# A two-stage float32 product of eight elements, its second stage in part by seven block products in place of eight

## The chip, the cores and the metric

The kernel runs on one core of one Trainium2 chip (trn2). The metric is device time in microseconds (us), the median of several runs. One execution of it is also taken by the hardware profiler, which gives the page and the trace read here.

## What is computed

There are NB = 8 batch elements of T = 256 tokens and D = 1024 channels, all in float32. Cut to what matters, with `w` the 1024 x 1024 weight that an id picks for each element out of eight:

```
y      = einsum('bsi,boi->bso', x, weight[adapter_ids])        # stage 1
base   = einsum('btd,od->bto', y, base_W) + base_b             # stage 2, the base
logits = einsum('btd,nd->btn', y, router_W) + router_b         # 15 router columns
probs  = softmax(logits); top 8 of 15, each added to its expert -> gate[b, t, e]
h      = einsum('btd,erd->bter', y, A)                         # 8 experts x 16 = 128 columns
out    = x + base + einsum('bter,eor->bto', h * gate, B) * 2.0
```

## The kernel before

**Split in two parts.** A float32 product is made of three passes in the type float32r. ScalarE (ACT) casts a raw tile to a high part, VectorE (DVE) subtracts that from the raw tile and gets the low part, and TensorE (PE) multiplies high by high, high by low and low by high into the same PSUM bank.

**Stage 1.** For each element, 8 chunks of 128 output channels (`stage1_chunk`, L540). A chunk is 8 pairs of matmuls, one over 512 columns (the weight's high part against the high and the low part of x, L546) and one over 256 (its low part against x's high part, L548), into `y_ps`. ACT then copies half of the bank to `y_part` (L300), DVE adds the two halves to `y_sum` (L468), ACT casts `y_hi` (L306), DVE makes `y_lo` (L397). The weights of a chunk are 512 KB; the SP queue loads them into one of four slots `w_raw`, as soon as DVE has made the low part of the chunk that was there (`w_lo_done`, L198). ACT casts them (L293), DVE makes `w_lo` (L385).

**Stage 2.** The shared matrix has AR + D = 144 + 1024 = 1168 columns: 128 of A, 15 of the router and one of padding, then the base. It lies in SBUF in two parts (`s2_hi`, `s2_lo`) for the whole run, and is cut in three groups of 384, 392 and 392 columns. `group` (L563) makes one group for one of the two token tiles of 128 tokens: 8 k-slices of three matmuls, 24 in all. `stage2` (L593) sets the order on PE:

```
group(b, 0, 0, ...); group(b, 1, 0, first).then_inc(ar_done, 1)
group(b, 0, 1, first); group(b, 0, 2, first)
pe.wait_ge(hw_done, b + 1)          # then the two transposes of hw
group(b, 1, 1, first)
pe.wait_ge(hwt_lo_done, b + 1)      # then lora_b for five groups, group(b, 1, 2), lora_b(1, 2)
```

When `ar_done` comes, DVE runs `routing` (L404): logits, softmax, top 8, gates, and `hw`, the gated A columns. PE transposes `hw`, ACT and DVE split it, and `lora_b` (L583) adds the product with B, 18 matmuls an element. DVE adds each group to `res` (`output`, L463), which holds x plus the bias (L448), and SP stores it.

**Order.** Every engine's program is written out by hand, for the first element, a hardware loop over elements 1 to 6, and the last. DVE's for an element (L471) is: for each chunk `y_sum`, a `w_lo`, `y_lo`; then the low parts of the next element's x (`x_lo`, L392), routing, the bias, `hwt_lo`, the output. The next element's x has a tile `x_raw` of its own, loaded at the element's start. In the first element the shared matrix is loaded piecewise through four slots `c_raw`, split by ACT (L285) and DVE (L379), and the first two chunks of stage 1 run in plain float32 (L560) straight from the raw tiles.

Of the kernel before, what the change touches and what calls it, by code (L numbers as in the profile page):

```python
# [19 lines left out]
C_SLOTS = 4  # L33
LORA_SCALE = 32.0 / 16.0
WARM_UP = 10
MARK = 3.0e38


def adaln_ffn_kernel(nc, xT, x, ids, wT, a_t, base_t, b_t, router_t, base_b, router_b, expert_map, out):
# [23 lines left out]
    with ExitStack() as ctx:  # L63
        def sb(name, shape, dt=F32):
            return ctx.enter_context(nc.sbuf_tensor(name, shape, dt))

        def sem(name):
            return ctx.enter_context(nc.semaphore(name))


# [615 lines left out]
```

## Time and profile before

| what | value |
|---|---|
| time, median of 3 runs | 422.53 us (422.02 to 422.95) |
| span of the profiled execution, first to last instruction | 421.1 us |
| PE busy | 413.3 us, 98% of the span |
| DVE busy | 220.0 us, 52% |
| ACT busy | 135.3 us, 32% |
| DMA queue, share of 16 engines | 43.4% |

The page gives the profiled execution by its span; the time of a run is taken around the program, and the median lies 1.4 us above the span. An element takes 50.7 us, of which stage 1 is some 22 and stage 2 some 28. Engines overlap: a busy share tells how full an engine is, not what the time waits for, and to see that one reads the idle time of the engine that is full. The notation is L for a line of the kernel, `out<-in` for the tiles, `<-` for who ended an idle time.

### The profile page before, as it was taken

How to read it: one execution, taken by the hardware profiler on the slowest of the kernel's cores; microseconds unless marked ns; L12 is line 12 of the kernel's file. 1: busy time of each engine (PE TensorE's matmuls, PEld its weight loads, DVE VectorE, ACT ScalarE, POOL GpSimd, SP SyncE). 2: the span in 40 equal slices, each digit the busy share in tenths (PEclk: the TensorE clock that was granted, in tenths of full speed). 3: DMA queues.
4: the chain of work that ended last, by engine and by line, in shares of the span. 5: the costliest groups of instructions: out<-in, count | busy, mean ns of one | idle time of the engine just before them, and what ended most of it. 6: DMA issues, size and time to landing. Idle time of an engine off the chain costs nothing.

```text
span 421.1 us, 6443 instructions
## 1 busy us (share of the span) xinstructions
PE 413.3 (98%) x2356; PEld 390.4 (93%) x2356; DVE 220.0 (52%) x438; ACT 135.3 (32%) x236; POOL 0.8 (0%) x8
## 2 busy tenths in 40 slices
PE   6989999999999999999999999999999999999997
PEld 5879998899988999899998999989998899988996
DVE  2577858654266623676227652366424655255232
ACT  3475534630055300561015600365004540053000
POOL 0000000000000000000000000000000000000000
PEclk8999999999999999999999999999999999999999
DMA  6876966930177203771057511574016740150002
GB/s 201 287 281 215 362 238 255 339 128 0 69 252 283 95 0 121 270 256 50 0 191 269 196 42 50 194 280 173 0 50 224 280 144 0 50 199 2 0 2 100
DMA packets 20093, 64.72 MB, mean 154 GB/s; under 512 B 2418, under 2 KB 6130, under 8 KB 19186
## 3 DMA queue, kind: packets, MB, share of 16 engines
q1 hardware_dynamic: 20082, 64.57, 43.4%
q8 instruction: 7, 0.11, 0.1%
q14 instruction: 4, 0.03, 0.0%
HBM read 56.18 MB, written 8.39 MB: 153 GB/s over the span
## 4 chain that ended last, share of the span: by engine, by line
PE 95%; DMA 2%; DVE 1%; SPq 0%; ACT 0%; issue 0%
PE y_ps L546 26%; PE s_ps L578 16%; PE s_ps L577 16%; PE s_ps L580 16%; PE y_ps L548 13%; DMA w_raw<-in_wT 2%; PE y_ps L560 2%; PE s_ps L589 2%; PE s_ps L588 2%; PE s_ps L590 2%; PE s_ps L605 0%; DVE w_lo L385 0%; ACT s_hi L285 0%; SPq L195 0%; SPq L191 0%
## 5 line engine op out<-in xcount | busy, mean ns | idle before, releaser
L546 PE MATMUL y_ps<-x_split,w_hi 128*128 128x512 f32 x496 | 172.7, 392 | 1.2 <-DVE w_lo L385 1.2
L548 PE MATMUL y_ps<-x_split,w_lo 128*128 128x256 f32 x496 | 139.1, 280 | 0.0
L577 PE MATMUL s_ps<-s_hi,y_hi 128*128 128x392 f32 (+1 forms) x384 | 131.2, 342 | 0.0
L578 PE MATMUL s_ps<-s_lo,y_hi 128*128 128x392 f32 (+1 forms) x384 | 130.4, 340 | 0.0
L580 PE MATMUL s_ps<-s_hi,y_lo 128*128 128x392 f32 (+1 forms) x384 | 130.0, 339 | 0.0
L546 PEld LDWEIGHTS y_ps<-x_split,w_hi 128*128 128x128 f32 x496 | 92.9, 187 | 21.6 <-DVE w_lo L385 1.5
L548 PEld LDWEIGHTS y_ps<-x_split,w_lo 128*128 128x128 f32 x496 | 94.0, 190 | 0.0
L385 DVE TENSOR_TENSOR w_lo<-w_raw,w_hi 128x1024 fp32r<-128x1024 f32 x62 | 75.2, 1215 | 1.4 <-ACT w_hi L293 1.4
L577 PEld LDWEIGHTS s_ps<-s_hi,y_hi 128*128 128x128 f32 x384 | 72.2, 188 | 0.3
L578 PEld LDWEIGHTS s_ps<-s_lo,y_hi 128*128 128x128 f32 x384 | 72.2, 188 | 0.0
L580 PEld LDWEIGHTS s_ps<-s_hi,y_lo 128*128 128x128 f32 x384 | 72.1, 188 | 0.0
L300 ACT COPY y_part<-y_ps 128x256 f32<-128x256 f32 x62 | 23.0, 371 | 148.5 <-PE y_ps L548 148.5
L293 ACT CAST w_hi<-w_raw 128x1024 fp32r<-128x1024 f32 x62 | 64.9, 1053 | 4.8 <-DMA w_raw<-in_wT 4.7
L468 DVE TENSOR_TENSOR y_sum<-y_ps,y_part 128x256 f32<-128x256 f32 x62 | 26.3, 424 | 59.6 <-ACT y_part L300 59.3
L463 DVE TENSOR_TENSOR res<-s_ps,res 128x392 f32<-128x392 f32 (+1 forms) x48 | 23.2, 510 | 57.0 <-PE s_ps L590 56.3
L397 DVE TENSOR_TENSOR y_lo<-y_sum,y_hi 128x256 fp32r<-128x256 f32 x64 | 26.8, 419 | 9.0 <-ACT y_hi L306 8.9
L306 ACT CAST y_hi<-y_sum 128x256 fp32r<-128x256 f32 x64 | 26.0, 407 | 12.8 <-DVE y_sum L468 7.9
L448 DVE TENSOR_TENSOR res<-res,bias 128x1024 f32<-128x1024 f32 x16 | 18.9, 1217 | 5.0 <-DMA res<-in_x 5.0
L321 ACT CAST hwt_hi<-s_ps 128x256 fp32r<-128x256 f32 x8 | 3.0, 375 | 54.6 <-PE s_ps L605 54.6
L392 DVE TENSOR_TENSOR x_split<-x_raw,x_split 128x1024 fp32r<-128x1024 f32 x14 | 16.6, 1220 | 2.0 <-ACT x_split L313 2.0
L452 DVE TENSOR_TENSOR hwt_lo<-s_ps,hwt_hi 128x256 fp32r<-128x256 f32 x8 | 3.4, 425 | 26.7 <-ACT hwt_hi L321 26.7
L589 PE MATMUL s_ps<-b_lo,hwt_hi 128*128 128x392 f32 (+1 forms) x48 | 15.3, 320 | 0.0
(46 smaller groups left out, 162.5 us busy)
## 6 DMA issues: line engine op xcount, KB each, us to landing
w_raw<-in_wT SPq DMA_DIRECT2D x63, 512.0 KB, 3.5
res<-in_x SPq DMA_DIRECT2D x16, 512.0 KB, 4.9
out<-res SPq DMA_DIRECT2D x15, 512.0 KB, 2.7
x_raw<-in_xT SPq DMA_DIRECT2D x7, 1024.0 KB, 5.5
c_raw<-in_base_t SPq DMA_DIRECT2D x8, 392.0 KB, 3.7
x_raw<-in_xT SPq DMA_DIRECT2D x4, 256.0 KB, 4.2
c_raw<-in_base_t SPq DMA_DIRECT2D x2, 480.0 KB, 7.4
w_raw<-in_wT SPq DMA_DIRECT2D x4, 128.0 KB, 4.4
```

What stands on the lines that cost most here:

```text
L293: nc.scalar.copy(w_hi[:, slot, :, :], w_raw[:, slot, :, :]).then_inc(w_hi_done, 1)
L306: nc.scalar.copy(y_hi[:, o, :], y_sum[:, o % 2, :]).then_inc(y_hi_done, 1)
L385: nc.vector.tensor_tensor(w_lo[:, slot, :, :], w_raw[:, slot, :, :], w_hi[:, slot, :, :], ALU.subtract).then_inc(w_lo_done, 1)
L397: nc.vector.tensor_tensor(y_lo[:, o, :], y_sum[:, o % 2, :], y_hi[:, o, :], ALU.subtract).then_inc(y_lo_done, 1)
L463: nc.vector.tensor_tensor(res[:, t, cols], s2_ps[:, g, t, skip:skip + OUT[g + 1] - OUT[g]], res[:, t, cols], ALU.add).then_inc(out_done, 1)
L468: nc.vector.tensor_tensor(y_sum[:, o % 2, :], y_ps[:, o % 2, 0:T], y_part[:, o % 2, :], ALU.add).then_inc(y_sum_done, 1)
L546: nc.tensor.matmul(y_ps[:, o % 2, :], w_hi[:, slot, k, :], x_split[:, k, :, :].rearrange("p s t -> p (s t)"), start=(k == 0), stop=False)
L548: mm = nc.tensor.matmul(y_ps[:, o % 2, 0:T], w_lo[:, slot, k, :], x_split[:, k, 0, :], start=False, stop=(k == KC - 1))
L577: nc.tensor.matmul(dst, hi, s2_hi[:, k, cols], start=(k == 0), stop=False)
L578: nc.tensor.matmul(dst, hi, s2_lo[:, k, cols], start=False, stop=False)
L580: mm = nc.tensor.matmul(dst, lo, s2_hi[:, k, cols], start=False, stop=(g == 0 and k == KC - 1))
L589: nc.tensor.matmul(dst, hwt_hi[:, t, :], b_lo[:, cols], start=False, stop=False, skip_group_check=skip)
```

## The change

**The base columns.** 288 of the 1024 base columns stay as they are, behind the 144 columns of A and router: `plain` (24 matmuls of 432 columns for each token tile). The other 736 are two halves N1 and N2 of 368. With the eight k-slices cut in two halves of four, and the tokens in two tiles, this is a 2 x 2 by 2 x 2 block product. From the second element on it is made by seven block products instead of eight (Winograd's form), each of 12 matmuls of 368 columns:

- on the left, sums of blocks of y: S1 = y10 + y11, S2 = S1 - y00, S3 = y00 - y10, S4 = y01 - S2 (here y10 is tile 1, first half of k), made by DVE in every element and split by ACT and DVE like y;
- on the right, sums of blocks of the base: T1 = B01 - B00, T2 = B11 - T1, T3 = B11 - B01, T4 = B10 - T2, made once, behind the first element;
- products that enter several outputs stay in a PSUM bank (`x_ps`) and are read by DVE between two products that add to it, so PE waits for DVE's `add` there.

The first element uses plain blocks: its blocks are B00, B10, T1 and B11, so that N2 is made as T1 and B11 products on one bank; it has the same columns as before.

**Bytes.** Raw tiles now lie on the bytes of the low parts: `w_raw` on `w_lo`, the next x on the low half of `x_split`, `y_sum` on `y_lo`. So a weight slot is free when PE is through with the chunk (`y_ps_done`), no longer when DVE is, and the next x is loaded when stage 1 is over.

**Order.** The y chunks come in the order 0, 4, 1, 5, ... and y is cast in pairs. The bias is added ahead of the routing.

The core of the diff:

```
-                    sp.wait_ge(w_lo_done, split(b, 3 + o))
-                    load_w(...)
+                    sp.wait_ge(y_ps_done, OC * b + c + 1)
+                    load_w(this if c + W_SLOTS < OC else nxt, (c + W_SLOTS) % OC)
...
+                if not last:
+                    load_x(b + 1)            # behind the last chunk, 2 x 512 KB
...
+            def sums(b, j):
+                nc.vector.tensor_tensor(s_raw[:, j, S1, :], y10, y11, ALU.add).then_inc(s1_done, 1)
+                nc.vector.tensor_tensor(s_raw[:, j, S3, :], y00, y10, ALU.subtract)
+                dve.wait_ge(s1_done, KH * (b - 1) + j + 1)
+                nc.vector.tensor_tensor(s_raw[:, j, S2, :], s_raw[:, j, S1, :], y00, ALU.subtract).then_inc(s_done, 1)
...
+            def fourth(b):
+                dve.wait_ge(ar_done, 2 * b + 1)
+                dve.wait_ge(s_lo_done, KH * (b - 1) + KH)
+                ... S4 in three operations of 512 elements, then fourth_hi on ACT, fourth_lo on DVE
...
+            def element(b, last=False):                      # DVE
+                for c in range(OC):
+                    make_y_sum(b, c)
+                    if c % 2:
+                        sums(b, c // 2)
+                        make_y_lo(b, c // 2)
+                    adapter_lo(b, c + 3)
+                    if c % 2:
+                        sums_lo(b, c // 2)
+                if isinstance(b, int) and b == 1:
+                    t2_lo()                                  # 1472 elements
+                    t34_lo()                                 # 2944 elements
+                add_bias(b)
+                fourth(b)
+                if not last:
+                    make_x_lo(b + 1)
+                fourth_lo(b)
+                stage2(b)          # routing_logits, add x_ps, routing_gates, the other adds
...
+            def stage2(b):                                   # PE
+                plain(b, 1)
+                plain(b, 0)
+                product(x_ps, y_block(0, 0), B00).then_inc(x_ps_done, 1)
+                pe.wait_ge(t_lo_done, 3)
+                product(z_ps, s_block(S1), T1).then_inc(z_ps_done, 1)
+                pe.wait_ge(x_added, x_adds(b, 1))
+                product(x_ps, s_block(S2), T2, begins=False).then_inc(x_ps_done, 1)
+                pe.wait_ge(hw_done, b + 1)
+                transposes()
+                product(w_ps, y_block(1, 0), B10)
+                pe.wait_ge(x_added, x_adds(b, 2))
+                product(x_ps, s_block(S3), T3, begins=False).then_inc(x_ps_done, 1)
+                pe.wait_ge(s4_lo_done, b)
+                product(z_ps, y_block(0, 1), B11, begins=False)
+                ... lora_b, then product(x_ps, y_block(1, 1), T4, begins=False)
```

Three places show what moves. **First, DVE in the loop over elements**, from the last low part of weights to the first use of the logits. Before:

```order
L385 TENSOR_TENSOR w_lo<-w_raw,w_hi 128x1024 [waits w_hi_done]
L391 ISA
L392 TENSOR_TENSOR x_split<-x_raw,x_split 128x4x256 [waits x_hi_done]
L391 REGISTER_ALU
L392 TENSOR_TENSOR x_split<-x_raw,x_split 128x4x256 [waits x_hi_done]
L407 REGISTER_ALU
L408 TENSOR_TENSOR logits<-s2_ps,router_bias 128x30 [waits ar_done]
```

Now:

```order
L487 TENSOR_TENSOR s_lo_70<-s_raw_71,s_hi_69 128x384 [waits s_hi_done]
L554 ISA
L555 TENSOR_TENSOR res_74<-res_74,bias_73 128x1024 [waits res_in0]
L555 TENSOR_TENSOR res_74<-res_74,bias_73 128x1024 [waits res_in1]
L490 ISA
L492 TENSOR_TENSOR y_sum_67<-y_hi_65,s_hi_69 128x4x128 [waits s_lo_done,ar_done]
L493 TENSOR_TENSOR s4_tmp_68<-y_lo_66,s_lo_70 128x4x128
L495 TENSOR_TENSOR y_sum_67<-y_sum_67,s4_tmp_68 128x4x128 [waits s4_part_done]
L464 TENSOR_TENSOR x_split_52<-x_raw_53,x_split_52 128x4x256 [waits x_hi_done]
L463 REGISTER_ALU
L464 TENSOR_TENSOR x_split_52<-x_raw_53,x_split_52 128x4x256 [waits x_hi_done]
L499 TENSOR_TENSOR y_lo_66<-y_sum_67,y_hi_65 128x4x128 [waits s4_hi_done]
L507 TENSOR_TENSOR logits_85<-pl_ps,router_bias_82 128x30 [waits ar_done]
```

Two additions of the bias and four operations for S4 now stand between the last low part and the logits.

**Second, PE in the same loop**, where the third group before, and the products on `z_ps` and `x_ps` now, begin behind a wait. Before:

```order
L580 MATMUL s2_ps<-s2_hi,y_lo 128x392
L566 REGISTER_ALU
L577 MATMUL s2_ps<-s2_hi,y_hi 128x392 [waits out_done]
```

Now:

```order
L816 ISA [waits t_lo_done]
L817 REGISTER_ALU [waits s_lo_done]
L761 MATMUL z_ps<-st_hi_57,s_hi_69 128x368 [waits z_added]
...
L819 REGISTER_ALU
L761 MATMUL x_ps<-st_hi_57,s_hi_69 128x368 [waits x_added]
...
L821 REGISTER_ALU
L781 MATMUL v_ps<-ident_80,hw_77 128x128 [waits v_added,hw_done]
```

`out_done` was a wait for the output of the element before; `x_added` is one for an `add` of this element.

**Third, DVE behind stage 1 of the first element**, from the last `y_lo` to `hwt_lo` (the rows of the routing left out). Now:

```order
L606 TENSOR_TENSOR st_lo_58<-hi_raw_60,st_hi_57 128x2x2x368 [waits blocks_hi_done]
...
L625 TENSOR_TENSOR hi_raw_60<-hi_raw_60 128x4x368 [waits mask_done]
L627 TENSOR_TENSOR st_raw_59<-st_raw_59,hi_raw_60 128x4x368 [waits t_done]
L555 TENSOR_TENSOR res_74<-res_74,bias_73 128x1024 [waits res_in0]
...
L542 TENSOR_TENSOR hw_77<-pl_ps,gate_n_96 128x256 [waits gate_done]
L464 TENSOR_TENSOR x_split_52<-x_raw_53,x_split_52 128x4x256 [waits x_hi_done] x2
L697 TENSOR_TENSOR b_lo_62<-b_raw_63,b_hi_61 128x1024 [waits b_hi_done]
L458 TENSOR_TENSOR w_lo_50<-w_raw_51,w_hi_49 128x1024 [waits w_hi_done] x3
L549 TENSOR_TENSOR hwt_lo_76<-v_ps,hwt_hi_75 128x256 [waits hwt_hi_done]
```

Before, `hw` was followed by `b_lo`, one half of x and `hwt_lo` at once:

```order
L440 TENSOR_TENSOR hw<-s2_ps,gate_n 128x256 [waits gate_done]
L379 TENSOR_TENSOR b_lo<-c_raw,b_hi 128x1024 [waits c_hi_done]
L392 TENSOR_TENSOR x_split<-x_raw,x_split 128x4x256 [waits x_hi_done]
L452 TENSOR_TENSOR hwt_lo<-s2_ps,hwt_hi 128x256 [waits hwt_hi_done]
```

The second half of x and the three low parts of weights moved ahead of `hwt_lo`, and block sums and the bias ahead of the routing.

## Rows read from the trace of the kernel before

**Rows 1.** The page: span, and busy time of each engine

```profile
span 421.1 us, 6443 instructions
PE 413.3 (98%) x2356; PEld 390.4 (93%) x2356; DVE 220.0 (52%) x438; ACT 135.3 (32%) x236; POOL 0.8 (0%) x8
```

**Rows 2.** The page: the chain that ended last, share of the span by engine

```profile
PE 95%; DMA 2%; DVE 1%; SPq 0%; ACT 0%; issue 0%
```

**Rows 3.** Stretches: length, then busy (count) of PE, PEld, DVE, ACT, POOL, clock, DMA

```profile
7.49:16.04 8.55, 8.55 (x32) 7.16 (x32) 3.11 (x5) 3.53 (x5) 0.00 (x0) 0.80 0.87 301
16.04:66.00 49.96, 48.77 (x279) 45.95 (x278) 36.82 (x71) 25.11 (x38) 0.00 (x0) 1.00 0.75 263
...
265.80:316.50 50.70, 50.70 (x294) 48.06 (x293) 26.18 (x52) 15.62 (x28) 0.00 (x0) 1.00 0.40 145
```

**Rows 4.** PE in time, one element: start us, us, line, operation, out<-in, count

```profile
237.32 0.33 PE L577 MATMUL s_ps<-s_hi,y_hi 128*128 128x384 f32 x1
...
245.71 0.34 PE L577 MATMUL s_ps<-s_hi,y_hi 128*128 128x392 f32 x1
...
261.03 0.34 PE L577 MATMUL s_ps<-s_hi,y_hi 128*128 128x392 f32 x1
...
265.11 0.34 PE L580 MATMUL s_ps<-s_hi,y_lo 128*128 128x392 f32 x1
...
265.82 0.40 PE L546 MATMUL y_ps<-x_split,w_hi 128*128 128x512 f32 x1
```

**Rows 5.** DVE in time, the same element

```profile
237.92 0.42 DVE L468 TENSOR_TENSOR y_sum<-y_ps,y_part 128x256 f32<-128x256 f32 x1 [0.88 <-ACT y_part L300]
...
240.72 2.36 DVE L392 TENSOR_TENSOR x_split<-x_raw,x_split 128x1024 fp32r<-128x1024 f32 x2 [0.34 <-ACT x_split L313]
...
245.92 0.19 DVE L408 TENSOR_TENSOR logits<-s_ps,router_bias 128x30 f32<-128x30 f32 x1 [2.83 <-PE s_ps L580]
...
247.00 0.18 DVE L422 TENSOR_REDUCE row_sum<-prob 128x2 f32<-128x30 f32 x1
...
248.96 2.35 DVE L448 TENSOR_TENSOR res<-res,bias 128x1024 f32<-128x1024 f32 x2
```

**Rows 6.** ACT in time, the same element

```profile
237.52 0.37 ACT L300 COPY y_part<-y_ps 128x256 f32<-128x256 f32 x1 [1.15 <-PE y_ps L548]
238.38 0.41 ACT L306 CAST y_hi<-y_sum 128x256 fp32r<-128x256 f32 x1 [0.49 <-DVE y_sum L468]
238.69 1.05 ACT L293 CAST w_hi<-w_raw 128x1024 fp32r<-128x1024 f32 x1
```

**Rows 7.** Groups by line and form: count, busy us, mean ns, idle before

```profile
L463 DVE TENSOR_TENSOR res<-s_ps,res 128x392 f32<-128x392 f32 x32 | 17.7, 564 | 30.4 <-PE s_ps L590 29.6
...
L492 DVE TENSOR_TENSOR x_split<-x_raw,x_split 128x512 fp32r<-128x512 f32 x4 | 2.7, 693 | 7.7 <-ACT x_split L341 7.7
...
L341 ACT CAST x_split<-x_raw 128x512 fp32r<-128x512 f32 x4 | 2.5, 618 | 5.2 <-DMA x_raw<-in_xT 5.2
```

**Rows 8.** DVE in time, first element

```profile
45.75 0.70 DVE L521 TENSOR_SCALAR expert_mask<-map_f 128x15 f32<-128x15 f32 x8
```

**Rows 9.** PE in time, first element

```profile
7.49 0.89 PE L560 MATMUL y_ps<-x_raw,w_raw 128*128 128x256 f32 x2 [2.13 <-DMA w_raw<-in_wT]
...
25.99 0.50 PE L546 MATMUL y_ps<-x_split,w_hi 128*128 128x512 f32 x1 [1.19 <-DVE w_lo L385]
...
34.42 0.34 PE L577 MATMUL s_ps<-s_hi,y_hi 128*128 128x384 f32 x1
...
63.02 0.40 PE L546 MATMUL y_ps<-x_split,w_hi 128*128 128x512 f32 x1
```

**Rows 10.** DMA issues: count, KB each, us to landing

```profile
w_raw<-in_wT SPq DMA_DIRECT2D x63, 512.0 KB, 3.5
res<-in_x SPq DMA_DIRECT2D x16, 512.0 KB, 4.9
...
x_raw<-in_xT SPq DMA_DIRECT2D x7, 1024.0 KB, 5.5
```

More of the change, by code:

```diff
@@ L32 @@
 F32_CHUNKS = 2
-C_SLOTS = 4
 LORA_SCALE = 32.0 / 16.0
@@ L273, in _ @@
+            store(0, 1, slice(0, D))
             with sp.Fori(1, NB - 1) as b:
@@ L466, in make_y_sum, with add @@
[L466 to L486 removed]
+            def add(t, cols, ps):
+                return nc.vector.tensor_tensor(res[:, t, cols], ps, res[:, t, cols], ALU.add)
@@ new lines, in _ @@
+            blocks_lo(0)
+            blocks_lo(1)
+            masks()
+            block_sums_1_2()
+            add_bias(0)
+            routing_logits(0)
+            routing_gates(0)
+            make_x_lo(1)
+            dve.wait_ge(b_hi_done, 1)
+            nc.vector.tensor_tensor(b_lo[:, :], b_raw[:, :], b_hi[:, :], ALU.subtract).then_inc(b_lo_done, 1)
+            for c in range(OC, OC + 3):
+                adapter_lo(0, c)
+            make_hwt_lo(0)
+            block_sums_3_4()
+            dve.wait_ge(res_biased, 2)
@@ new lines, in _ @@
+            dve.wait_ge(z_ps_done, 1)
+            add(0, N2, z_ps[:, 0:NH]).then_inc(z_added, 1)
+            dve.wait_ge(x_ps_done, 1)
+            add(1, N2, x_ps[:, 0:NH]).then_inc(x_added, 1)
+            dve.wait_ge(w_ps_done, 1)
+            add(0, N1, w_ps[:, 0:NH]).then_inc(w_added, 1)
+            add_plain(0)
+            t1_lo()
+            dve.wait_ge(v_ps_done, 1)
+            add(1, N1, v_ps[:, 0:NH]).then_inc(v_added, 1)
+            element(1)
+            with dve.Fori(2, NB - 1) as b:
@@ new lines, in product @@
+            def product(ps, y_block, block_of, begins=True, wait_blocks=0):
+                dst = ps[:, 0:NH]
+                hi, lo = y_block
+                for j in range(KH):
+                    if wait_blocks and j % 2 == 0:
+                        pe.wait_ge(blocks_lo_done, j + wait_blocks)
+                    nc.tensor.matmul(dst, hi(j), st_hi[:, j, block_of, :], start=begins and j == 0, stop=False, skip_group_check=not begins)
+                    nc.tensor.matmul(dst, hi(j), st_lo[:, j, block_of, :], start=False, stop=False, skip_group_check=not begins)
+                    mm = nc.tensor.matmul(dst, lo(j), st_hi[:, j, block_of, :], start=False, stop=(j == KH - 1),
+                                          skip_group_check=not begins)
+                return mm
@@ new lines, in y_block, with s_block, lora_b @@
+            def y_block(half, t):
+                return [(lambda j, y=y: y[:, half * KH + j, t * P:(t + 1) * P]) for y in (y_hi, y_lo)]
+            def s_block(i):
+                return [(lambda j, s=s: s[:, j, i, :]) for s in (s_hi, s_lo)]
+            def lora_b(t, dst, cols, begins=False):
+                skip = not begins
+                nc.tensor.matmul(dst, hwt_hi[:, t, :], b_hi[:, cols], start=begins, stop=False, skip_group_check=skip)
+                nc.tensor.matmul(dst, hwt_hi[:, t, :], b_lo[:, cols], start=False, stop=False, skip_group_check=skip)
+                return nc.tensor.matmul(dst, hwt_lo[:, t, :], b_hi[:, cols], start=False, stop=True, skip_group_check=skip)
```

780 lines of the change are left out of this document (454 added, 326 removed).

## The prediction

> **What bounds the kernel now.** I read the page's busy times first: PE is busy for 413.3 of 421.1 us [rows 1], and the chain that ended last is 95% PE [rows 2]. Then the stretches: in an element of the loop PE is busy for 50.70 of 50.70 us at clock 1.00 (2.4 GHz), DVE for 26.2, ACT for 15.6 [rows 3]. So PE's columns set the time, and DVE has slack on average. The change takes columns from PE and hands DVE work, with waits for it, so the question is at what moment DVE's work is asked for. The view for that is the engines in order of time around the end of stage 1, at 237.32 us, which I call zero below [rows 4 to 6].
>
> **What it takes from PE.** Stage 2 lasts from 237.32 to 265.82, 28.50 us, so stage 1 takes 22.20 [rows 3, 4]. Its 48 matmuls of 384 columns take 8.39 us, 0.1748 each, and 23 of 392 columns take 4.08, 0.1774 each [rows 4]. That is 0.453 ns a column; I scale by it. A matmul of 432 columns then takes 0.1956, one of 368 takes 0.167, one of 288 some 0.131. Now: 48 x 0.1956 + 84 x 0.167 + 12 x 0.167 + 6 x 0.131 + 0.26 for the transposes = 9.39 + 14.03 + 2.00 + 0.79 + 0.26 = 26.47. Before, the same sum gives 8.39 + 17.03 + 2.13 + 0.66 + 0.26 = 28.47, as measured. So **2.0 us less in each of seven elements, 14.2 us in all**, if PE never waits. The first element keeps its columns.
>
> The Trainium skill (TensorE: Matmul & The Clock Gate, section on the back-to-back issue gap) has a matmul at full clock cost its columns at 2.4 GHz and some 2.5 ns. The trace disagrees by 12 ns on 392 columns (166 against 177). By that figure the seven elements would save 4416 columns and 12 matmuls each, 13.1 us, and the forecast would be 1.1 us higher.
>
> **What DVE must do in the loop before PE may go on.** The sixth product, S2 by T2, adds to the bank that the `add` on `x_ps` must first have read (L819 in the change). PE gets there after two `plain` and two products: 9.39 + 24 x 0.167 = 13.4 us. DVE's path to that `add`:
> - y_sum of the last chunk runs from 0.60 to 1.02 [rows 5]. Three sums of 128 elements: the nearest rows are 0.19 for 30 elements and 0.42 for 256 [rows 5], so I estimate 0.29 each; one waits for another, and y_lo starts at 1.8, over two chunks at once (512 elements: 0.69, or 0.61 to the next start [rows 7]), to 2.4.
> - ACT casts y at 1.06 (0.52 to the next start) and then weights for 1.05 [rows 6, 7]. So w_lo runs from 2.7 to 3.8 (two of this size take 2.36, 1.14 apart [rows 5]), the low part of the sums (384 elements, 0.48) to 4.3.
> - The bias, twice 1.14 [rows 5], to 6.5. S4: two operations of 0.61 and a third that waits for the second, to 8.5.
> - ACT casts S4 (0.5) and the first half of x (1.05), to 10.15. DVE takes both halves of x (2 x 1.14) to 12.4, S4's low part 0.6 to 13.0.
> - Logits to the first sum over probabilities take 247.00 - 245.92 = 1.08 [rows 5], to 14.1. The `add` of 368 elements takes 0.54 (0.564 for 392 [rows 7]), to 14.7.
>
> So **PE waits 14.7 - 13.4 = 1.3 us in each loop element**. Bounds: 0 if the small operations cost nothing and the casts overlap better, 2.5 if each of some ten new waits costs 0.1 more. The rest of the routing takes 248.96 - 247.00 = 1.96 [rows 5] and ends at 16.6; PE is through S2 by T2 at 16.7, so the transposes don't wait. What is late next is covered: the `add` on x_ps for S3 ends near 17.5 and is wanted at 18.9; hwt_lo at 18 is wanted at 23. S4's low part at 13.0 is wanted at 20.9. The next x is issued behind one weight load after zero; landed one after the other they take 3.5 + 5.5 = 9.0 us [rows 10], and ACT is ready for it at 9.1. In pieces a quarter as long that could cost up to 1 us; I take 0.
>
> Net for elements 2 to 6: 5 x (-2.03 + 1.3) = -3.65. The last has no next x (2.3 us of DVE and ACT's two casts gone from the path), so it does not wait: -2.0.
>
> **Element 1** has the block sums' low parts in the same path, ahead of the bias: 1472 and 2944 elements. From 512 to 1024 elements a DVE operation grows by 1.02 ns an element [rows 5, 7], so 1.6 and 3.1 us, with ACT's cast ending at 4.4 just ahead: the path moves by 4.85. PE waits 6.15: -2.03 + 6.15 = +4.1.
>
> **Element 0.** Stage 1 ended at 34.42, its chunk 5 having waited to 25.99 for weights [rows 9]. Now DVE and ACT have the plain part's split (1152 elements, 1.3 and 1.1 us) ahead of y_sum 4, on which chunk 6 waits: w_lo of 6 to about 28.2, split to 29.5, y_sum to 29.9, where chunk 6 could start near 28.3. I take +1.1, bounds -1.0 (A and router are loaded earlier, the old wait goes) and +2.5. In stage 2, counted from its start, DVE's work ends: four low parts of blocks of 1472 elements from 3.0 to 9.4, masks 0.9 (0.70 for the eight comparisons [rows 8]) to 10.3, two block sums to 13.6, bias to 15.9, routing (3.04 [rows 5]) to 18.9. PE wants `hw` after 9.39 + 48 x 0.167 = 17.4: it waits 1.5. Then two halves of x, b_lo and three w_lo, 6 x 1.14, and hwt_lo: 26.15. PE wants it at 18.95 + 0.26 + 4.0 = 23.2: it waits 2.9. Before, this stage took 28.6 without a stop [rows 9], so +4.4.
>
> **The clock.** Before, PE stood still for 2.1 us behind its warm-up, up to 7.49 [rows 9], and over the next 8.55 us the mean clock is 0.80, part of it thus at half clock (1.2 GHz), which loses 0.2 x 8.55 = 1.7. A stop of 1.2 us ahead of 25.99 [rows 9] left it at 1.00 [rows 3]. The 6.15 us of element 1 is far longer than the first, the 1.3 us stops are like the second. I put **+1.7** for one stretch at half clock; bounds 0 and 3.4 (element 0's 2.9 as well). The Trainium skill (TensorE: Matmul & The Clock Gate, Part 1) says that the throttled clock is the default state and activity releases it, a rule that speaks against any change that makes PE stop; both rows agree with it.
>
> **Sum.** 421.1 + 1.1 + 4.4 + 4.1 - 3.65 - 2.0 + 1.7 = 426.7 us of span. The tail behind the last matmul is alike (one add, one small store). The median stood 1.4 above the span: **428.1 us**, 5.6 slower. A measurement of this kernel tells some 0.2% (0.85 us) from no change.
>
> **Rivals.**
> - *DVE is in time in the loop.* If its path is shorter by 1.3 us, elements 2 to 6 never wait, and if the clock stays up too: 426.7 - 6.5 - 1.7 + 1.4 = 419.9, faster. For it: DVE is half idle. Against: every large operation on the path is priced by its own row. It decides from 1.3 us on; in between lie results near no change. Chance 0.16, of it 0.03 for the full 14.2 us (about 408), which would need element 0 and 1 covered too.
> - *Each short stop brings half clock.* Five more losses of up to 1.7: near 436. The skill's rule would allow it; the 1.2 us stop of before speaks against. 0.09.
> - *Weights come late.* A slot is now free when PE is through, three chunks (8.3 us) ahead. Landing 3.5, or 4.9 as for `res` beside other loads [rows 10], cast 1.05, low part 1.2, and about 1 us in both queues make 6.8 to 8.2. A wait of 1 us in each of seven elements gives 435. 0.08.
> - *The products are not fewer.* If PE's records don't drop by 84 from 2356, the saving is absent: 442. 0.01.
> - The forecast, with its own range of 425 to 431.5: 0.58. Near no change: 0.08.
>
> Faster 0.16, same 0.08 and slower 0.76 come from these; the range, 419.8 to 434.5, takes in the first rival and stops short of the second.
>
> **What would show it.** PE: 2272 matmuls; a wait on x_ps by the `add` (L558) of about 1.3 us in elements 2 to 6 and 6 us in element 1; waits for hw and hwt_lo of 1.5 and 2.9 in element 0; no wait for w_lo in the loop; one dip of the clock. Loop elements of 50.0 us, the last 48.7. If they take 48.7 as well, DVE's path is mis-sized; if they exceed 50.7, a new wait stands in stage 1 or the clock is down.

## The result and the profile after

The changed kernel takes **431.54 us** (median of 4 runs, 429.67 to 432.55), the kernel before 422.74 beside it (422.02 to 423.70). The ratio is 1.0204, 95% interval 1.0171 to 1.0236: slower by 2.0%, and the whole interval lies above 1. The forecast was 428.1 with a range of 419.8 to 434.5.

The page of the changed kernel, from its longest run of the four: span, busy times, clock in 40 slices, and chain by engine. They answer to [rows 1, 2].

```profile
span 430.7 us, 6373 instructions
...
PE 404.3 (94%) x2272; PEld 373.5 (87%) x2272; DVE 295.6 (69%) x577; ACT 154.9 (36%) x238; POOL 0.8 (0%) x8
...
PEclk9999999999599999999999999999999999999999
...
PE 61%; DVE 21%; ACT 6%; issue 6%; DMA 5%; SPq 1%; DVEq 0%; ACTq 0%
```

PE makes 2272 matmuls where it made 2356, and is busy for 404.3 us instead of 413.3. But its share of the span fell from 98% to 94% and its share of the chain from 95% to 61%, with 21% for DVE. One slice of the clock row shows a 5. Ahead of the products on `x_ps` (L761) PE stood idle for 12.5 us, until the `add` (L558) was done. The waits of PE, in total, times and the longest:

```profile
PE x_ps L761 <- DVE res L558: 12.5, 6, 6.8
PE y_ps L726 <- DVE y_sum L470: 2.9, 3, 1.4
PE z_ps L775 <- DVE hwt_lo L549: 2.8, 1, 2.8
...
PE v_ps L781 <- DVE hw L542: 1.6, 1, 1.6
```

Stretches, columns as in [rows 3]: stage 2 of the first element, stage 1 and stage 2 of element 1, and element 3:

```profile
35.20:68.48 33.28, 28.92 (x167) 27.99 (x165) 30.91 (x51) 16.35 (x16) 0.00 (x0) 1.00 0.42 162
68.48:91.95 23.47, 22.47 (x130) 19.41 (x130) 15.45 (x28) 12.26 (x21) 0.00 (x0) 1.00 0.66 225
91.95:128.48 36.53, 29.72 (x154) 28.67 (x153) 24.56 (x47) 6.99 (x11) 0.00 (x0) 0.86 0.18 59
178.92:228.93 50.01, 48.95 (x282) 45.44 (x282) 35.31 (x72) 17.92 (x29) 0.00 (x0) 1.00 0.42 147
```

Piece by piece, by the times at which PE begins each in both kernels (before: [rows 3, 9] and its other elements):

| piece | before, us | after, us | difference | forecast |
|---|---|---|---|---|
| up to stage 2 of element 0 | 34.42 | 35.20 | +0.78 | +1.1 |
| stage 2 of element 0 | 28.60 | 33.28 | +4.68 | +4.4 |
| element 1 | 50.70 | 60.00 | +9.30 | +4.1, and 1.7 for the clock |
| element 2 | 50.71 | 50.44 | -0.27 | -0.73 |
| elements 3 to 6 | 4 x 50.70 | 4 x 50.00 | -2.80 | -2.92 |
| element 7 and tail | 53.87 | 51.77 | -2.10 | -2.0 |
| span | 421.1 | 430.7 | +9.6 | +5.6 |

The table puts what is missing in one place, element 1. Here is DVE at the end of its stage 1, which ends at 91.95:

```profile
93.63 0.42 DVE L470 TENSOR_TENSOR y_sum<-y_ps,y_sum 128x256 f32<-128x256 f32 x1
...
97.43 1.69 DVE L646 TENSOR_TENSOR st_lo<-st_raw,st_hi 128x1472 fp32r<-128x1472 f32 x1
99.03 3.22 DVE L641 TENSOR_TENSOR st_lo<-st_raw,st_hi 128x2944 fp32r<-128x2944 f32 x1
102.17 2.35 DVE L555 TENSOR_TENSOR res<-res,bias 128x1024 f32<-128x1024 f32 x2
...
108.08 2.36 DVE L464 TENSOR_TENSOR x_split<-x_raw,x_split 128x1024 fp32r<-128x1024 f32 x2 [1.63 <-ACT x_split L367]
```

The low parts of T2 and of T3 and T4 (1.69 and 3.22 us) stand ahead of the bias, S4 and x. And PE from there on, as matmuls and as stretches:

```profile
112.54 0.68 PE L761 MATMUL x_ps<-st_hi,s_hi 128*128 128x368 f32 x1 [6.81 <-DVE res L558]
113.01 0.51 PE L762 MATMUL x_ps<-st_lo,s_hi 128*128 128x368 f32 x1
113.32 0.51 PE L763 MATMUL x_ps<-st_hi,s_lo 128*128 128x368 f32 x1
```

```profile
112.50:118.60 6.10, 6.06 (x20) 5.98 (x21) 3.22 (x11) 0.37 (x1) 0.00 (x0) 0.50 0.00 0
```

PE stands still for 6.81 us. Then the matmuls start 0.31 us apart instead of 0.167, and the granted clock is 0.50 (1.2 GHz) for 6.10 us (in the stretch behind it, up to 121.00, the mean is 0.99). The clock fell while PE stood still, not when it started again: the mean is 1.00 from 106.00 to 108.00, 0.60 in the next 2 us and 0.50 behind them.

The steady element does what the forecast had said step by step. Its stage 1 ends at 201.11:

```profile
205.39 2.36 DVE L555 TENSOR_TENSOR res<-res,bias 128x1024 f32<-128x1024 f32 x2
...
211.31 2.36 DVE L464 TENSOR_TENSOR x_split<-x_raw,x_split 128x1024 fp32r<-128x1024 f32 x2 [1.63 <-ACT x_split L367]
...
214.19 0.18 DVE L507 TENSOR_TENSOR logits<-pl_ps,router_bias 128x30 f32<-128x30 f32 x1
...
215.18 0.53 DVE L558 TENSOR_TENSOR res<-x_ps,res 128x368 f32<-128x368 f32 x1
```

### The profile page after: what moved, and what is told of

Read it like the earlier page. It is cut to its first block, busy times and chain, and to the rows that moved or that the text cites. A ratio compares the mean times of both kernels' runs of the same rounds, so it can differ in the third digit from the quotient of the medians.

```text
span 430.7 us, 6373 instructions
## 1 busy us (share of the span) xinstructions
PE 404.3 (94%) x2272; PEld 373.5 (87%) x2272; DVE 295.6 (69%) x577; ACT 154.9 (36%) x238; POOL 0.8 (0%) x8
## 4 chain that ended last, share of the span: by engine, by line
PE 61%; DVE 21%; ACT 6%; issue 6%; DMA 5%; SPq 1%; DVEq 0%; ACTq 0%
PE y_ps L726 22%; PE y_ps L728 11%; DMA w_raw<-in_wT 5%; PE x_ps L761 4%; PE x_ps L763 4%; PE x_ps L762 4%; DVE w_lo L458 3%; ACT w_hi L357 3%; DVE res L555 3%; DVE x_split L464 3%; ACT x_split L367 1%; PE y_ps L738 1%; PE z_ps L762 1%; PE z_ps L761 1%; PE z_ps L763 1%
## 5 line engine op out<-in xcount | busy, mean ns | idle before, releaser
L349 ACT COPY y_sum<-y_ps 128x256 f32<-128x256 f32 x62 | 23.1, 372 | 115.7 <-PE y_ps L728 115.7
L470 DVE TENSOR_TENSOR y_sum<-y_ps,y_sum 128x256 f32<-128x256 f32 x62 | 26.1, 421 | 30.3 <-ACT y_sum L349 29.7
L749 PE MATMUL pl_ps<-pl_hi,y_hi 128*128 128x432 f32 x128 | 46.0, 359 | 0.0
L750 PE MATMUL pl_ps<-pl_lo,y_hi 128*128 128x432 f32 x128 | 45.8, 358 | 0.0
L751 PE MATMUL pl_ps<-pl_hi,y_lo 128*128 128x432 f32 x128 | 45.8, 358 | 0.0
L558 DVE TENSOR_TENSOR res<-x_ps,res 128x368 f32<-128x368 f32 x29 | 15.6, 537 | 41.1 <-PE x_ps L763 26.9
L761 PE MATMUL x_ps<-st_hi,s_hi 128*128 128x368 f32 x56 | 19.9, 355 | 12.5 <-DVE res L558 12.5
L474 DVE TENSOR_TENSOR y_lo<-y_sum,y_hi 128x512 fp32r<-128x512 f32 x32 | 22.2, 693 | 6.4 <-ACT y_hi L353 2.7
L749 PEld LDWEIGHTS pl_ps<-pl_hi,y_hi 128*128 128x128 f32 x128 | 24.1, 188 | 1.6 <-DVE y_lo L474 0.3
L751 PEld LDWEIGHTS pl_ps<-pl_hi,y_lo 128*128 128x128 f32 x128 | 24.1, 188 | 1.0
L750 PEld LDWEIGHTS pl_ps<-pl_lo,y_hi 128*128 128x128 f32 x128 | 24.0, 188 | 0.9
L761 PEld LDWEIGHTS x_ps<-st_hi,s_hi 128*128 128x128 f32 x56 | 11.0, 197 | 14.3 <-DVE res L558 14.3
L763 PE MATMUL x_ps<-st_hi,y_lo 128*128 128x368 f32 x64 | 21.1, 330 | 0.0
```

The lines of the kernel that those rows point to most:

```text
L470: nc.vector.tensor_tensor(y_sum[:, o, :], y_ps[:, c % 2, 0:T], y_sum[:, o, :], ALU.add).then_inc(y_sum_done, 1)
L749: nc.tensor.matmul(dst, hi, pl_hi[:, k, :], start=(c == 0), stop=False)
L750: nc.tensor.matmul(dst, hi, pl_lo[:, k, :], start=False, stop=False)
L751: mm = nc.tensor.matmul(dst, lo, pl_hi[:, k, :], start=False, stop=(c == KC - 1))
L761: nc.tensor.matmul(dst, hi(j), st_hi[:, j, block_of, :], start=begins and j == 0, stop=False, skip_group_check=not begins)
L763: mm = nc.tensor.matmul(dst, lo(j), st_hi[:, j, block_of, :], start=False, stop=(j == KH - 1), skip_group_check=not begins)
```

## Experiments

Each is the changed kernel with one edit, unless said otherwise. Ratios are to the kernel before, run beside it. Each profile is of one execution.

My theory at this point: PE's saving is real, and DVE pays for more than it in two places, once (elements 0 and 1) and in every element (1.3 us). The rivals were that the block sums are not what costs, but the layout or the weights; that the half clock and not the stop is the loss; and that any work moved out of the one stop comes back as another.

### 1. The low parts of T2, T3 and T4 ahead of element 1

```
@@ DVE, end of element 0
             add(1, N1, v_ps[:, 0:NH]).then_inc(v_added, 1)
+            t34_lo()
+            t2_lo()
@@ DVE, element
-                if isinstance(b, int) and b == 1:
-                    t2_lo()
-                    t34_lo()
```

ACT's cast of T2 moves likewise, behind that of T3 and T4.

> Edit: the high and low parts of T2, T3 and T4 are made ahead of element 1 (behind the last add of element 0) instead of behind its stage 1. Theory (DVE's path to the first add on x_ps sets PE's long stop in element 1; the stop brings the half clock): the path of element 1 shortens by 4.8 us, the wait of PE on x_ps there falls from 6.8 to about 2.0 us, the slow matmuls behind it are at full clock again (-2.9 us), span 430.7 - 4.8 - 2.9 = 423.0 us. Elements 2 to 7 stay at 50.0 and 48.8. Rival (late weights and transfers on shared bytes make the stop): the wait stays above 5 us and the span above 428.

Median 424.01 us (10 runs, 421.66 to 427.88), ratio 1.0039 (1.0001 to 1.0077). The profile, with a span of 419.8, is of the fastest of the ten. Stage 1 and stage 2 of element 1:

```profile
67.51:90.18 22.67, 22.43 (x129) 19.51 (x129) 21.22 (x32) 13.82 (x22) 0.00 (x0) 1.00 0.62 231
90.18:117.99 27.81, 26.73 (x154) 26.04 (x153) 18.41 (x43) 5.48 (x9) 0.00 (x0) 1.00 0.23 78
```

Stage 2 of element 1 fell from 36.53 to 27.81 us, and the clock stays at 1.00. The two operations cost 4.9 us of DVE and took 8.7 us of PE's time where they stood. Half a microsecond came back in stage 1 (22.67 against 22.2). PE's six waits on `x_ps` are now all short, 1.1 us at most. The 10 runs lie 6.2 us apart. Experiment 4 tells one thing that may do that, but not all of it is the clock: the runs of 421.66 and of 424.37 us both have a mean granted clock of 1.000.

### 2. x split behind hwt_lo

```
@@ DVE, element
-                if not last:
-                    make_x_lo(b + 1)
                 fourth_lo(b)
-                stage2(b)
+                stage2(b, last)
@@ DVE, stage2
                 make_hwt_lo(b)
+                if not last:
+                    make_x_lo(b + 1)
```

> Edit: DVE makes the low parts of the next x behind hwt_lo instead of between S4 and its low part. Theory (DVE's path sets the stops): the path loses 2.3 us of work and the 1.6 us that DVE waits for ACT's cast of x, so the waits of 1.1 to 1.5 us in elements 2 to 6 vanish (-6.0 us, elements of 48.8), the 6.8 us of element 1 become about 3 (-3.9), and the half clock goes or stays (-2.9 or 0): span 418 to 421 us. Rival (PE is held by the products or by transfers, DVE only ends late together with them): elements stay at 50.0, span 427 or more. Second rival: x is now late for the next element's stage 1, a wait on x_split of up to 1 us an element.

Median 419.23 us (10 runs, 418.08 to 421.19), ratio 0.9929 (0.9901 to 0.9957): **faster than the kernel before**, by 0.7%, with the whole interval below 1. The profile is of the fastest run. Stage 2 of element 1, and element 3:

```profile
90.03:121.06 31.03, 28.32 (x155) 27.55 (x153) 23.16 (x45) 6.71 (x10) 0.00 (x0) 0.95 0.20 70
169.76:218.44 48.68, 48.68 (x282) 45.49 (x281) 35.39 (x72) 17.83 (x29) 0.00 (x0) 1.00 0.44 151
```

In the loop PE is busy for 48.68 of 48.68 us: the saving of 2.0 us an element is there whole, and the wait of 1.3 us is gone once the two halves of x are off DVE's path. They had 2.36 us of work and 1.63 of waiting for ACT there, more than the 1.3. Whether moving the bias or S4 would have ended the wait as well was not tried. The same edit took the stop of element 1 from 6.81 to 2.71 us. That shorter stop also ended in a stretch at lower clock:

```profile
106.30:110.30 4.00, 3.96 (x15) 3.88 (x16) 2.73 (x10) 0.05 (x1) 0.00 (x0) 0.60 0.00 0
```

### 3. The stop of element 1 filled

42 matmuls of 368 columns that nobody reads, on a bank that is free there, ahead of the wait for the `add`, in element 1 alone. They are extra work.

```
                 product(z_ps, s_block(S1), T1).then_inc(z_ps_done, 1)
+                if fill:
+                    pe.wait_ge(w_added, b)
+                for i in range(fill):
+                    nc.tensor.matmul(w_ps[:, 0:NH], y_hi[:, 0, 0:P], st_hi[:, 0, T2, :], start=True, stop=True)
                 pe.wait_ge(x_added, x_adds(b, 1))
```

> Edit: 42 matmuls of 368 columns that nothing reads (7.0 us of work, on the free bank w_ps) fill PE's stop in element 1; PE's program has element 1 written out. Nothing is saved but the clock. Theory (the stop itself brings the half clock of the 20 matmuls behind it): the clock stays at 1.00 through the element, span 430.7 - 2.9 = 427.8 us, and element 1 takes some 57 us instead of 60.0. Rival (the slow matmuls have another cause, the engine's restart or DVE's traffic): their stretch keeps taking 3 us more, span 430.7.

Median 430.24 us (429.36 to 432.22), ratio 1.0188 (1.0121 to 1.0254).

```profile
92.13:125.62 33.49, 33.49 (x197) 33.08 (x195) 23.17 (x45) 6.81 (x10) 0.00 (x0) 1.00 0.20 66
```

```profile
111.09 0.53 DVE L558 TENSOR_TENSOR res<-x_ps,res 128x368 f32<-128x368 f32 x1
```

The 42 matmuls last as long as the changed kernel's stop with its restart, 7.0 us, and stage 2 of element 1 takes 33.49 us instead of 36.53: the 3.0 us between are what the half clock cost, apart from the stop. The clock row of the change says the same: 6.10 us at 0.50 are a loss of 3.05. The medians differ by only 1.3 us, less than expected, and the intervals of the two ratios overlap. Two things work against the gain: in the profile stage 1 of element 0 took 1.45 us longer here, and the `add` began 18.96 us behind the end of stage 1 (92.13) where it began 20.00 behind it in the change, so the fill lasts some 1 us longer than this kernel's own stop would have. So the 3.0 us are read from the stage, not from the median.

### 4. The same order with eight products

Without sums of blocks: layout, queues and order of the change, but the products of the first element in every element (the place of T1 then holds B01 throughout). DVE still makes the first two block sums, unread, so that the first element keeps its stops.

```
-                product(x_ps, y_block(0, 0), B00).then_inc(x_ps_done, 1)
-                product(z_ps, s_block(S1), T1).then_inc(z_ps_done, 1)
-                product(x_ps, s_block(S2), T2, begins=False).then_inc(x_ps_done, 1)
+                product(z_ps, y_block(0, 0), T1)
+                product(z_ps, y_block(1, 0), B11, begins=False)
+                product(x_ps, y_block(0, 1), T1)
+                product(x_ps, y_block(1, 1), B11, begins=False)
...
```

> Edit: the layout, order of chunks, shared bytes and casts in pairs of the change are kept, but all elements use the eight plain block products of the first one; no sums of blocks of y in any element, T3, T4 and the splits of the block sums are not made (T1 and T2 still are, unused). Theory (the layout costs nothing in the loop, the seven products save 2.0 us of PE and give most of it back in waits for DVE): elements 1 to 7 take 50.7 us each with no wait but a few tenths, element 0 stays at 68.5, span 68.5 + 354.9 + 3.0 = 426.4 us. Rival (the shared bytes make weights late in general): elements above 51 us with waits on w_lo or y_sum in stage 1, span above 429.

Median 428.27 us (427.57 to 430.45), ratio 1.0132 (1.0062 to 1.0203). Stage 2 of element 0, then element 3:

```profile
34.08:68.95 34.87, 30.52 (x167) 29.59 (x165) 26.59 (x48) 12.67 (x14) 0.00 (x0) 0.95 0.40 157
...
170.37:221.09 50.72, 50.72 (x294) 47.52 (x293) 26.34 (x48) 16.10 (x24) 0.00 (x0) 1.00 0.41 145
```

Loop elements are back at 50.7 us, as before the change and without a wait: bytes shared by raw and low parts cost nothing in the loop, so the rival of late weights is out there. What is left over the kernel before is stage 2 of element 0: 34.87 instead of 28.60. Of these 6.3 us 4.3 are the two waits of the change, and most of the rest is the clock. The two waits are as long in this kernel as in the changed one (1.59 and 2.75 us against 1.59 and 2.77), yet there the clock stays up behind them and here it does not (33.28 us for the stage there, so 1.6 more here):

```profile
61.00:63.00 2.00, 2.00 (x8) 2.00 (x7) 1.08 (x2) 0.00 (x0) 0.00 (x0) 0.50 0.00 0
63.00:66.00 3.00, 3.00 (x17) 3.00 (x17) 1.46 (x3) 0.00 (x0) 0.00 (x0) 0.78 0.24 97
```

PE's program is the same in both there. DVE's differs behind `hwt_lo`, for T3 and T4 are not made here, so these two profiles alone don't exclude the program as the cause. The kernels of experiments 1 and 8 do, for all engines have the same program in element 0 there. With the same stop of 2.8 us stage 2 took 33.31 us at clock 1.00 in experiment 1, and 34.83 and 36.09 us in two profiles of the kernel of experiment 8. So **a stop of 2.8 us costs at times the stop alone and at times 1.6 to 2.8 us more**, and what decides between them stays open.

### 5. The first element in another order

```
@@ DVE, behind stage 1 of element 0
             masks()
-            block_sums_1_2()
-            add_bias(0)
             routing_logits(0)
             routing_gates(0)
-            make_x_lo(1)
             ...
+            add_bias(0)
+            make_hwt_lo(0)
+            block_sums_1_2()
+            make_x_lo(1)
             for c in range(OC, OC + 3):
                 adapter_lo(0, c)
-            make_hwt_lo(0)
             block_sums_3_4()
```

ACT's `make_hwt_hi` moves ahead of the three casts of weights.

> Edit: in element 0 alone, DVE makes T1 and T2 and adds the bias behind hwt_lo instead of ahead of the routing, and hwt_lo ahead of the next x and weights; ACT casts hwt_hi ahead of the three next w_hi. Theory (the stops of 1.6 and 2.8 us in element 0 are DVE's order): both vanish, stage 2 of element 0 takes 28.8 to 29.2 us instead of 33.3, span 430.7 - 4.3 = 426.4 us; the next element's work on DVE is not late. Rival: PE's products of element 0 are held by the blocks' splits and loads, stage 2 stays above 31.5 us. Second rival: what moved behind hwt_lo makes the x or the weights of element 1 late, and its start waits for as much as was won.

Median 432.44 us (432.04 to 433.28), ratio 1.0216 (1.0168 to 1.0264). Stage 2 of element 0, then stage 1 of element 1:

```profile
36.03:64.52 28.49, 28.49 (x166) 28.11 (x165) 22.61 (x42) 12.67 (x14) 0.00 (x0) 1.00 0.41 156
64.52:93.70 29.18, 24.52 (x129) 20.83 (x129) 24.13 (x39) 16.03 (x22) 0.00 (x0) 0.94 0.58 192
```

```profile
PE y_ps L726 <- DVE y_sum L470: 7.1, 4, 3.9
```

Both waits of element 0 are gone, and its stage 2 takes 28.49 us. Stage 1 of element 1 takes 29.18 instead of 23.47: it now waits for y_sum, which DVE makes behind the block sums. 4.8 us are won in the one stage and 5.7 lost in the other (7.0 against the 22.19 of experiment 2). That is much what the second rival said. This order did not take the wait away, it moved it behind the block sums.

### 6. Experiments 1, 2 and 5 together, and the splits later as well

The second of these moves the split of A and router, and of the plain part, one chunk later in stage 1 of the first element.

> Edit: t_early, x_behind and first_order together. Theory: the parts add, 411.7 - 4.3 = 407.4 us of span, some 408.5 to 409.5 in the median, faster than both kernels by 3%. Rival: the block sums that moved behind hwt_lo in element 0, with T2 to T4 behind the last add, reach into stage 1 of element 1 and hold y_sum: a wait of 1 to 3 us there, span 409 to 411.

> Edit: all3, and in stage 1 of element 0 the splits of A, router and the plain columns come one chunk later. Theory: the waits of PE for y_sum there (1.7 us in the change) shrink to under 0.5, span 406.2 us, median about 407.5. Rival: the weights' landing sets these waits, and they only move to the next chunk: same as all3 within 0.5 us.

Medians 421.97 us (ratio 0.9967, 0.9933 to 1.0001) and 421.53 (0.9960, 0.9933 to 0.9987), 13 to 14 us above what was expected. Both medians lie above that of experiment 2 alone, though the intervals of the ratios overlap, and clearly above the 415.86 of experiments 1 and 2 without 5 (experiment 8). The later splits did not take away the wait for y_sum in stage 1 of element 0 either: 1.45 us in the first kernel, 1.47 in the second. Stage 1 of element 1 in the second:

```profile
63.87:96.82 32.95, 24.52 (x129) 21.13 (x129) 29.67 (x42) 17.49 (x23) 0.00 (x0) 0.84 0.49 173
```

Stage 1 of element 1 takes 32.95 us, with one wait of 8.4 us for y_sum: more was pushed into it, and more came back there, with the clock at 0.84.

### 7. The block sums on GpSimd

Experiment 2, and all work on T1 to T4 (four sums, three low parts) taken from DVE and given to GpSimd (POOL), which had been idle; then the same with `hwt_lo` early, as in experiment 5.

```
-                nc.vector.tensor_tensor(r_t1, r01, r00, ALU.subtract).then_inc(t_done, 1)
+                nc.gpsimd.tensor_tensor(r_t1, r01, r00, ALU.subtract).then_inc(t_done, 1)
...
```

> Edit: x_behind, and all the work on the block sums (T1 to T4 and their low parts, 11,776 elements a partition) is done by GpSimd (POOL) instead of DVE. Theory (in elements 0 and 1 DVE's total work is the bound: first_order and all3 only moved the stops to y_sum): DVE has 11.2 us less in these two elements. In element 0 the wait for hw (1.6) goes and that for hwt_lo falls from 2.8 to about 1.2, stage 2 takes 29.8 us; element 1 has no stop on x_ps and takes 48.7 to 49.5 us instead of 53.2. Span 416.3 - 3.5 - 4.0 = 408.8 us, median near 410.5, faster than before by 3%. Rival: POOL is so slow (over 5 us for 1472 elements) that T1's or T4's low part is late for PE in element 1, a wait on t_lo_done there; span above 413. Second rival: POOL and DVE slow each other down, DVE's operations of 1024 elements take over 1.3 us.

> Edit: pool_sums, and in element 0 hwt_hi and hwt_lo come ahead of the next x and weights, the bias behind b_lo. Theory: with 11.2 us off DVE the reorder that gave nothing before now keeps what it wins: the last wait for hwt_lo (1.2) goes and y_sum in element 1 is not late by more than 0.5 us; span 407.6 us, median near 409. Rival: as in first_order, the wait moves to y_sum in stage 1 of element 1 and the span is that of pool_sums or more.

Medians 433.78 us (ratio 1.0258, 1.0220 to 1.0296) and 428.12 (1.0125, 1.0076 to 1.0174). In the first, stage 2 of element 0 takes 52.27 us, of which PE waits 10.1 for hwt_lo and 6.9 for hw, and its mean clock is 0.84. Element 1 takes 49.97 us, near the 48.7 to 49.5 expected. In the second kernel the stage takes 37.09 us and stage 1 of element 1 another 30.95, where 22.2 are its work. POOL and DVE side by side in the first:

```profile
35.33 3.38 POOL L841 TENSOR_TENSOR hi_raw<-hi_raw 128x1472 f32<-128x1472 f32 x1 [33.78 <-DMA st_raw<-in_base_t]
38.78 3.71 POOL L843 TENSOR_TENSOR st_raw<-st_raw,hi_raw 128x1472 f32<-128x1472 f32 x1
48.93 3.37 POOL L848 TENSOR_TENSOR st_raw<-st_raw,hi_raw 128x1472 f32<-128x1472 f32 x1 [6.43 <-DVE st_lo L611]
52.25 3.36 POOL L849 TENSOR_TENSOR st_raw<-st_raw 128x1472 f32<-128x1472 f32 x1
64.82 4.36 POOL L853 TENSOR_TENSOR st_lo<-hi_raw,st_hi 128x1472 fp32r<-128x1472 f32 x1 [9.21 <-ACT st_hi L445]
69.13 7.37 POOL L857 TENSOR_TENSOR st_lo<-st_raw,st_hi 128x2944 fp32r<-128x2944 f32 x1
```

```profile
36.59 2.67 DVE L474 TENSOR_TENSOR y_lo<-y_sum,y_hi 128x512 fp32r<-128x512 f32 x1 [0.69 <-ACT y_hi L353]
39.18 4.86 DVE L608 TENSOR_TENSOR st_lo<-hi_raw,st_hi 128x1472 fp32r<-128x1472 f32 x1
43.97 1.68 DVE L611 TENSOR_TENSOR st_lo<-st_raw,st_hi 128x1472 fp32r<-128x1472 f32 x1
...
48.96 7.06 DVE L619 TENSOR_SCALAR expert_mask<-map_f 128x15 f32<-128x15 f32 x8
56.06 2.36 DVE L555 TENSOR_TENSOR res<-res,bias 128x1024 f32<-128x1024 f32 x2
...
64.75 12.83 DVE L458 TENSOR_TENSOR w_lo<-w_raw,w_hi 128x1024 fp32r<-128x1024 f32 x3
```

A y_lo of 0.69 us takes 2.67 and ends 0.5 us behind POOL's first operation. The first low part of a block takes 4.86 where the next, with POOL at rest, takes 1.68. Eight comparisons of 15 elements take 7.06 us instead of 0.70 [rows 8], and end 0.4 us behind POOL's two operations beside them; three w_lo take 12.83 instead of the 3.49 of the changed kernel. Between them, with POOL at rest, the bias takes its 2.36. A y_sum at 35.48, with one input in PSUM, takes its usual 0.42 beside POOL's first operation. The work was not taken off DVE: DVE stood still for most of it, and longer, for POOL takes 3.4 us where DVE takes 1.69. This is the second rival. The Trainium skill (SBUF — State Buffer, section "Who interferes with whom") says that a DVE instruction with two inputs in SBUF contends with a GpSimd instruction that reads SBUF, and the one that comes second is held for all of it. The trace agrees for the low parts. The comparisons have one tensor as input; the Trainium skill, in the same section, lists `tensor_scalar` among the operations that can take the shared ports. That this is what held them is not shown.

### 8. Experiments 1 and 2 together

> Edit: t_early and x_behind together. Theory: each took its own part of DVE's path, 4.8 and 3.9 us in element 1, and PE's stop there (6.8 in the change, 2.7 left in x_behind, 1.1 in t_early) is gone; elements 1 to 7 all take 48.7 us and no clock is lost: span 67.8 + 7 x 48.7 + 3.0 = 411.7 us, the whole 14 us of columns saved in the loop. Rival (another wait stands right behind the first): elements of 49.3 or more.

One run, 415.96 us, with 48.68 us in elements 2 to 6. Stage 2 of element 0 took 34.83 us, again with the clock down behind the stop:

```profile
61.00:67.00 6.00, 6.00 (x28) 6.00 (x29) 6.00 (x8) 2.92 (x2) 0.00 (x0) 0.72 0.07 29
```

Then the same kernel in six runs:

> The two edits that shortened the stop of element 1 and of the steady elements, together: the sums of T2, T3 and T4 made ahead of element 1, and x's low half split behind hwt_lo. If each keeps what it gave alone, as the single look at this pair showed (span 414.1 us), the runs have a median of about 416.5 us, a ratio to the kernel before of 0.983 to 0.988, with 48.7 us in elements 2 to 6 and no wait of x_ps for res anywhere. If the work that both push into the first element's end comes back as a wait of y_sum in element 1, as it did when the block sums were moved, the pair is no better than the x edit alone: a median of 419 us and a ratio of 0.992 or above.

**Median 415.86 us (6 runs, 414.85 to 417.39), ratio 0.9835 (0.9803 to 0.9868).** Element 0 from its stage 2 on, stage 1 and 2 of element 1, element 3:

```profile
34.86:70.95 36.09, 31.74 (x166) 30.82 (x165) 30.92 (x51) 17.97 (x17) 0.00 (x0) 0.91 0.41 158
70.95:93.93 22.98, 22.73 (x129) 19.49 (x129) 20.99 (x32) 12.12 (x20) 0.00 (x0) 1.00 0.64 226
93.93:120.40 26.47, 26.47 (x155) 26.08 (x153) 18.65 (x43) 5.37 (x9) 0.00 (x0) 1.00 0.24 84
169.08:217.76 48.68, 48.68 (x282) 45.50 (x281) 35.41 (x72) 17.87 (x29) 0.00 (x0) 1.00 0.43 151
```

Element 1 has no stop left in stage 2 (26.47 us, all busy). Some of the moved work did come back, 0.8 us in its stage 1. The profiled execution is the longest of the six. Its stage 2 of element 0 took 36.09 us, for the clock was down behind the stop of 2.75 us:

```profile
61.00:64.00 3.00, 2.74 (x9) 2.77 (x10) 3.00 (x3) 0.00 (x0) 0.00 (x0) 0.50 0.00 0
64.00:67.00 3.00, 3.00 (x13) 3.00 (x12) 3.00 (x7) 2.60 (x2) 0.00 (x0) 0.50 0.04 15
```

## Why the prediction was right, and where it was not

**What PE saves: right.** 2.0 us an element were forecast, and 50.70 - 48.68 = 2.02 are measured (experiments 2 and 8). The scaling by 0.453 ns a column held. By the issue gap that the Trainium skill gives (TensorE: Matmul & The Clock Gate, section on the back-to-back issue gap) the estimate would be 13.1 / 7 = 1.87, and the trace is 0.15 above that.

**The stop in the loop: right.** Forecast 1.3 us, measured 50.00 - 48.68 = 1.32 in elements 3 to 6. The last add was to begin 14.1 us behind the end of stage 1; it began at 215.18 - 201.11 = 14.07. DVE's work on x began 10.2 us behind it, where the forecast has ACT's cast end at 10.15.
Element 2 took 0.44 more than the others, its stop being 1.50 us of idle time where theirs is 1.06; why is open.

**Element 0: right in its mechanism and size.** Waits of 1.59 and 2.77 us against 1.5 and 2.9, stage 2 +4.68 against +4.4, of which 0.3 is what two restarts cost beyond the idle time. Experiment 5 takes both waits away by the order on DVE and ACT alone. In stage 1 the wait for y_sum behind the plain part's split was forecast as 1.6 us and is 1.45 (at 29.48), and +0.78 stands against +1.1. That this sum agrees so well is in part luck: eight other profiles with the same program up to there reach stage 2 at 34.08 to 36.65 us, and the kernel before had its first chunks at a mean clock of 0.80 [rows 3] where the changed kernel had 1.00 (7.45 to 15.82), which the forecast had not counted.

**Element 1 was too small by 3.5 us, and is where the sum failed.** The term was "+4.1" and "+1.7 for one stretch at half clock"; measured is +9.3. It divides so:
- Half clock: 36.53 us of stage 2 less 26.49 of work leaves 10.04, of which experiment 3 gives 3.0 to the clock. The term was 1.7, from a stretch in which PE's mean clock was 0.80. Here it was at 0.50 for 6.10 us. The row I took didn't show a whole stretch of that length at the lower level. +1.3.
- The stop: 7.04 in place of 6.15 (6.81 of it idle, the rest in the restart). DVE came out of stage 1 later, y_sum of the last chunk at 1.68 us behind its end where I had 0.60. +0.9.
- Stage 1 of element 1: 23.47 in place of 22.20, +1.3. ACT waited 3.35 us for weights once, at 86.27, and y_sum came late for PE behind that:

```profile
86.27 1.05 ACT L357 CAST w_hi<-w_raw 128x1024 fp32r<-128x1024 f32 x1 [3.35 <-DMA w_raw<-in_wT]
```

The last two are the rival "weights come late" for a single chunk, not in each element. In the forecast it had a price of 1 us in each of seven elements or nothing. They belong to this execution more than to the change. The kernels of experiments 2 and 3 have the same program up to the end of this stage; they take 22.19 and 22.18 us for it, y_sum of the last chunk comes at 0.60 and 0.61, as forecast, and in experiment 3 the add begins 1.04 us earlier than in the changed kernel. Taken from the stop of 6.81 us, that leaves an estimate of 5.8 of idle time, or 6.0 with the restart, where 6.15 were forecast. So the stop was priced well, the half clock was not, and why one load came late in one of three profiles stays open.

**The rivals.** "DVE is in time" is false by 1.32 us an element; experiment 2 makes it true, with 419.2 us close to the 419.9 written for it. That closeness is in part luck: the same edit also shortens the stop of element 1, which the rival had left whole. Element 1 still keeps 4.5 us of loss there, and the whole 14 are not reached. "Each short stop brings half clock" is false for stops of 1.1 us: the clock is 1.00 in elements 3 to 6. "The products are not fewer" is false by the count of 2272.

**The sum.** The mechanism was right in each step. The error of 3.4 us in the median is nearly that of element 1 in the profile, but the profile is of the longest of four runs (429.67 to 432.55), and 2.2 us of its element 1 are the late load; how the other three runs divide is not on record. The value lay in the upper part of the range. The range had taken 0 to 3.4 for the clock of elements 0 and 1; experiments 4 and 8 show that its upper part is real, for the stop of element 0 brings its own loss in some executions. The profiled run of the changed kernel had none of it in element 0.

**What stays open.** The best kernel still loses 6.2 to 7.5 us in stage 2 of element 0 (two profiles), behind hw and hwt_lo. Reordering there did not pay, for the wait moved into the next stage, and POOL did not either. Giving part of the block sums to ACT was not tried.

## What to carry to other kernels

Where the full engine gets less work and a half-idle one gets more, don't compare the totals. Find the moment when the full engine first needs the result, and count what the other engine has in its queue ahead of it: here two operations that nobody wanted for another 15 us (x's low half) cost 1.3 of the 2.0 us that the loop gains in each element, and moving them behind the wanted one made the change pay. Work that is done once must be placed where the full engine isn't behind it on the same queue; if that engine's queue is full there, reordering can merely move the stop, as it did in experiment 5. A stretch in which that engine has slack would be the place to look for, which no run here tried for the block sums themselves.

## What was not expected of the hardware

- GpSimd and VectorE did not work side by side on tensors in SBUF: DVE's operations with both inputs there, and comparisons with one, took 2.67 instead of 0.69, 4.86 instead of 1.68 and 7.06 instead of 0.70 us beside POOL's (experiment 7). One with an input in PSUM took its usual 0.42.
- A stop of PE of 6.81 us was followed by 6.10 us at clock 0.50, and the clock had fallen while PE stood still. One of 2.71 us was followed by 4.00 us at a mean of 0.60 (experiment 2), and one of 2.75 to 2.77 us by none (the changed kernel), by a short one (experiment 4), by a mean of 0.72 over 6 us or by 0.50 over nearly 6 us (experiment 8, one kernel profiled twice). Stops of 1.1 us were followed by none. The length of a stop of this size doesn't tell what follows. That the Trainium skill has activity release the throttled clock (TensorE: Matmul & The Clock Gate, Part 1) agrees with all of these and doesn't tell them apart.
